# Last layer of a four-layer graph network: GpSimd paced by landed gathers instead of by marks from TensorE

## The reference, cut to what matters

```python
h = relu(edge_feat @ W1 + b1)                       # e x 64
w = (h @ W2 + b2).reshape(e, 4, 8, 8)               # e x 256
s_e = s[src]; v_e = v[src]                          # the gathered row: 8 + 24 numbers
m0 = ALPHA*(einsum(s_e*sh0, w_000) + C110*einsum(v_e, sh1, w_110))
m1 = ALPHA*(einsum(s_e, sh1, w_011) + einsum(v_e*sh0, w_101))
out0 = segment_sum(m0, dst) + SI_SCALE*(s @ si_w0)  # and out1 likewise
```

## Time and profile before

| | us |
|---|---|
| three runs | 7781.98, 7791.23, 7857.09 |
| median | 7791.23 |
| the profiled execution's own time | 7864.66 |
| its span in the profile | 7862.8 |
| last layer, first gather to the end of the last chunk | 4118.3 to 7849.8 |

### The profile page before, as it was taken

One profiled execution on the slowest core, in us unless ns is written; L12 is line 12 of the kernel. 1 busy time (PEld: TensorE's weight loads), 2 busy tenths in 40 slices (PEclk: granted clock), 3 DMA queues, 4 the chain that ended last, 5 costly groups with the idle time before them and its releaser, 6 DMA issues.

```text
span 7862.8 us, 118188 instructions
## 1 busy us (share of the span) xinstructions
PE 5606.6 (71%) x38929; PEld 4302.4 (55%) x38930; DVE 4286.2 (55%) x8297; ACT 3000.2 (38%) x7294; POOL 3946.9 (50%) x4168
## 2 busy tenths in 40 slices
PE   7477777777777775665674677777776777777677
PEld 3276777667666664333333455555555555555555
DVE  3355556665565561111103666666666666666677
ACT  4344444444444441000003444444444444444446
POOL 2355555555555555555204555555555555555553
PEclk6577777877877776776685667777776667776777
DMA  9433334444444447877880000000000000000000
GB/s 303 152 144 130 143 134 151 167 160 156 155 166 164 151 162 253 287 270 264 260 261 13 20 20 18 20 20 20 20 20 20 19 20 20 20 20 20 20 21 19
DMA packets 596643, 865.44 MB, mean 110 GB/s; under 512 B 170833, under 2 KB 418706, under 8 KB 579474
## 3 DMA queue, kind: packets, MB, share of 16 engines
q1 hardware_dynamic: 363858, 385.79, 15.5%
q10 hardware_dynamic: 99520, 406.06, 13.1%
q0 software_dynamic: 133120, 71.57, 4.9%
HBM read 455.19 MB, written 406.85 MB: 110 GB/s over the span
## 4 chain that ended last, share of the span: by engine, by line
PE 44%; another core or an unknown queue 18%; issue 16%; ACT 11%; DVE 8%; DMA 2%; ACTq 1%; DVEq 0%; SPq 0%
PE psum L1116 17%; PE psum L1066 9%; PE psum L1288 5%; PE psum L1174 5%; PE psum L1297 4%; ACT arena L768 3%; ACT arena L912 3%; ACT arena L798 2%; DVE arena L1970 2%; DVE arena L1956 2%; DVE arena L1948 2%; PE psum L1206 1%; DMA rel_table<-arena 1%; ACT arena L902 1%
## 5 line engine op out<-in xcount | busy, mean ns | idle before, releaser
L628 POOL DMA_INDIRECT gathered<-x_rows,idx x2048 | 1950.5, 952 | 2014.5 <-PE psum L1066 651.2
L628 POOL DMA_INDIRECT gathered<-rel_table,idx x2048 | 1933.6, 944 | 1664.4 <-issue 591.7
L1297 PE MATMUL psum<-w,arena 65*128 65x256 f32 x4096 | 1173.2, 439 | 331.5 <-DVE arena L1948 289.0
L797 ACT COPY arena<-psum 128x512 f32<-128x512 f32 x1024 | 603.4, 589 | 1552.0 <-PE psum L1116 1111.8
L1297 PEld LDWEIGHTS psum<-w,arena 65*128 65x128 f32 x4096 | 892.7, 225 | 497.3 <-DVE arena L1948 313.9
L1288 PE MATMUL psum<-arena,w 32*65 32x512 f32 x1024 | 575.5, 1061 | 656.1 <-ACT arena L896 398.2
L1066 PEld LDWEIGHTS psum<-arena 128*128 128x128 f32 x4096 | 885.2, 246 | 225.3 <-issue 203.8
L1116 PE MATMUL psum<-arena 64*128 64x128 f32 x8192 | 692.7, 326 | 420.7 <-ACT arena L798 253.2
L1066 PE MATMUL psum<-arena 128*128 128x184 f32 x4096 | 961.4, 398 | 3.9 <-DVE arena L1973 2.7
L1116 PE MATMUL psum<-table_out 64*128 64x128 f32 x8192 | 746.8, 349 | 239.5 <-ACT arena L798 173.6
L1116 PEld LDWEIGHTS psum<-arena 64*128 64x128 f32 x8192 | 630.9, 231 | 473.7 <-issue 250.2
(11 more groups left out here) (225 smaller groups left out, 5853.8 us busy)
## 6 DMA issues: line engine op xcount, KB each, us to landing
adj<-arena ACTq DMA_DIRECT2D x128, 2048.0 KB
arena<-adj SPq DMA_DIRECT2D x93, 2048.0 KB
counts<-arena ACTq DMA_DIRECT2D x128, 512.0 KB
arena<-counts SPq DMA_DIRECT2D x64, 1024.0 KB, 11.5
arena<-adj SPq DMA_DIRECT2D x40, 1024.0 KB
rel_table<-table_out ACTq DMA_DIRECT2D x32, 1024.0 KB
rel_table<-arena ACTq DMA_DIRECT2D x32, 1024.0 KB
gathered<-rel_table,idx POOLq DMA_INDIRECT x2048
```

The source lines that it names most:

```text
L628: pool.indirect_dma_start(gathered[:, s, j, :], None, rows[l], bass.IndirectOffsetOnAxis(ap=idx[:, s, j:j + 1], axis=0),).then_inc(group_i ...
L797: act.copy(w_to, made[:, 1]).then_inc(w_out, 1)
L1297: mm = pe.matmul(pair[g % 2][:, WN * q:WN * q + WN], hidden[:, s % 2, q, P * g:P * g + P], w2[:, :], start=True, stop=True)
```

## The change

The last layer's marks are taken out: `MARKS_3`, `MARK_TILES_3`, `CUTS_3` and `LEAD_3`, PE's five increments in every two chunks, and POOL's five waits for them. In their place POOL waits twice a chunk, ahead of its gathers 0 and 8, until the group of four gathers issued last has landed. Ahead of gather 8 that is group 1 of the same slot, ahead of gather 0 group 3 of the slot before. The amounts waited for are kept in eight registers, raised by 64 after each wait. The 64 gathers of the first round, the wait for `idx_in` ahead of each chunk, and the first layer's marks are as before.

```diff
-MARKS_3 = [({2}, (), {1}, {2}), ((), (), (), ())]
-MARK_TILES_3 = [(), (1, 9)]
-CUTS_3 = [0, 6, 12, 19, 25]
-LEAD_0, LEAD_LATE, LEAD_3 = 6, 6, 7
+RESTS_3 = (0, 8)
+LEAD_0, LEAD_LATE = 6, 6
...
+                def rows_landed(s, rest):
+
+                    last = (s - (rest == 0)) % SLOTS, (rest - 1) % TILES
+                    pool.wait_ge(group_in[last[0]][last[1] // GROUP], pool.snap(landed[s, rest]))
+                    pool.reg_add(landed[s, rest], landed[s, rest], 16 * GROUP)
+
+                def rests_3(s):
 
                     def pace(j):
 
-                        if s % 2 * TILES + j in CUTS_3:
-                            mark_passed()
+                        if j in RESTS_3:
+                            rows_landed(s, j)
                     return pace
...
-                        gather_chunk(3, s, marks_3(s))
+                        gather_chunk(3, s, rests_3(s))
...
-                    if q in marks:
-                        mm.then_inc(pe_mark, 1)
...
-                        mm = scatter(3, (s - 1) % SLOTS, (range(5), range(5, 11), range(11, TILES))[g - 1],
-                                     marks=MARK_TILES_3[s % 2])
+                        mm = scatter(3, (s - 1) % SLOTS, (range(5), range(5, 11), range(11, TILES))[g - 1])
```

More of the change, by code:

```diff
@@ L660, in marks_late @@
                         mark_passed()
-                def marks_3(s):
+                landed = {(s, rest): pool.alloc_register(f"landed_{s}_{rest}") for s in range(SLOTS) for rest in RESTS_3}
+                def rows_landed(s, rest):
[3 more added lines that the diff above has]
+                def rests_3(s):
                     def pace(j):
-                        if s % 2 * TILES + j in CUTS_3:
-                            mark_passed()
+                        if j in RESTS_3:
+                            rows_landed(s, j)
                     return pace
@@ L683, in _ @@
                     gather(2)
-                pool.reg_mov(mark, ROUNDS * by_round + MARKS_LATE * LATE + len(CUTS_3) * SLOTS // 2 + 1 - LEAD_3)
+                for s in range(SLOTS):
+                    for rest in RESTS_3:
+                        pool.reg_mov(landed[s, rest], 16 * GROUP * (1 + (s > 0 or rest > 0)))
                 pool.wait_ge(rows_out[2], 16)
@@ L1289, in hidden_units, with edge_weights @@
                               start=True, stop=True, tile_position=(F * q, 0)).then_inc(hidden_made, 1)
-            def edge_weights(c, s, g, marks):
+            def edge_weights(c, s, g):
                 if g == 0:
@@ L1307, in chunk3 @@
                 for g in range(GROUP):
-                    edge_weights(c, s, g, MARKS_3[s % 2][g])
+                    edge_weights(c, s, g)
                     if g == 1 and following:
```

## The result

| | before | changed |
|---|---|---|
| median of four runs each, us | 7792.19 | 7248.74 |
| lowest to highest, us | 7781.98 to 7857.09 | 7204.37 to 7264.39 |
| the profiled execution, us | 7864.66 | 7251.99 |

The changed kernel takes 0.9275 of the time of before, 95% interval 0.9225 to 0.9324: 543 us less on the chip of this measurement. On another chip the same kernel is slower than before by 8%; that is the second half of this document.

What follows compares the result with a forecast made beforehand. No engine was full; POOL's back-to-back gathers were taken to delay PE's semaphores. Chunks falling from 28.33 to 24.6 us, times 124, saved 463 us: 7402 profiled, about 7329 us as median, range 7130 to 7900.

Steps and rivals of the forecast that it cites:

- The state of things: Last layer: back-to-back POOL gathers delay PE's semaphores from about 5 us into a stretch until 1.7 to 2.6 us behind it.
- not the cause: Rival: PE's results are late for another reason and the gathers only coincide; 7791 us, chance 0.07.
- A stretch of eight and its pause clear: Last layer: eight gathers hold PE's semaphores 6.4 us instead of 12 to 13, and a 1.85 us pause just clears them.
- not cleared: Rival: 1.85 us is too short, a chunk's two stretches merge into one of about 21 us; 8740 us, chance 0.23 wholly or often.
- The pause: POOL's wait ahead of gathers 0 and 8: 1.05 us landing, 0.05 increment, 0.75 going on, 1.85 us in all.
- The upper bound of the prediction, 25.2: POOL's cycle in us a chunk if each pause took 2.9 us instead of 1.85.
- The reading that POOL has slack: Last layer: POOL's 23.1 us a chunk lies under the period, so nobody waits for its later gathers.
- How much of the hold-up a chunk feels: Last layer: DVE idles 4.8 us before group 2, repeating every 24.1 to 24.2 us; 24.6 us a chunk taken.
- The alternation of 21.6 and 37.9 us: Successive chunk periods of the kernel before, the long one holding two hold-up waits; the forecast was 24 to 25 us without it.
- The increments at zero: PE's five mark increments in two chunks ride on matmuls issued anyway; removal worth zero, at most 31 us for all 310.
- The sum: Last layer: (28.33 - 24.6) × 124 = 463 us off the profiled 7864.7, 7402; less 73 for the median, about 7329 us.

Runs made afterwards that it cites:

- stretches of sixteen: Changed kernel without its two waits a chunk, or with one, ahead of gather 0: 8212.49 and 8232.65 us on chip B, beside 7804.87 for the kernel before.
- B: Chip of four edits of the changed kernel: no pauses 8212.49, one pause 8232.65, gathers left out 6811.63, marks' increments kept 7260.99 us; kernel before 7804.87.
- A: Chip of the main result: changed kernel 7248.74 us beside 7792.19 for the kernel before; may be one of the other four chips.
- E: Chip of two edits of the changed kernel: waits for the group before 8385.16 us, ratio 1.0567; stretches of twelve 7811.15 us, ratio 0.9852.
- C: Chip of four edits of the changed kernel: four pauses 6605.11, first-round pauses too 6163.96, waits for the group before 5699.50, stretches of twelve 6047.43 us; kernel before 5700.81.
- D: Chip where the changed kernel ran again, unedited: 6149.80 us; with waits for the group before: 5696.00 us; kernel before 5703.32 us.
- The twelves: Changed kernel with three waits in two chunks, stretches of 12, 12 and 8 gathers: 6047.43 us (ratio 1.0620) on C, 7811.15 us (0.9852) on E.

## Why the prediction came out right, and where it did not

The forecast was 7329 us in 7130 to 7900, the result 7248.74. Point by point:

**The state of things: right for this chip.** Gathers back to back hold up PE's updates from some way into a stretch until 1.7 to 2.6 us behind it. The 5 us is a rough figure. In the changed kernel 290 of the 307 late updates are of matmuls that end over 5 us into a stretch. But of the recorded updates of matmuls that end 5 to 7 us in, less than a third are late, and of those 8 to 11 us in, six in seven. The prediction spoke of PE's updates alone; ACT's are late too, mostly in the stretches of sixteen (above), in those of eight 39 of 467, by up to 1.5 us. With the gathers gone the updates come at once and 449 us more are saved on the same chip (B: 7261 us with the marks' increments kept, 6812 without gathers), and with no or too short pauses the period is 31.2 to 31.8 us. The rival *not the cause* falls here, and its 7791 us with it. The rule of the Trainium skill (page "SBUF — State Buffer", section "Who interferes with whom") is that only VectorE and GpSimd contend and that TensorE never waits on anyone. It speaks of ports, and no trace here shows a port; what fails on A, B and E is what the prediction drew from it, that the gathers cannot delay PE's hand-offs. On C and D the traces agree with it.

**A stretch of eight and its pause clear: right, and narrowly.** The largest doubt, *not cleared* at 0.23, did not come true for eights: 1.99 us is as late as all but a few updates come, and the pause is 2.11. At the 1.85 us that the prediction had put down, 46 of the 307 late updates would have come after the pause's end. The twelves show the rival's mechanism. Its price was mis-sized: the prediction had merged two stretches into 36 us a chunk and 8740 us, the run without pauses has 31.29 and 8212 us. The 36 had counted a hold-up to 2.3 us behind a stretch that starts 2.3 after the release, with both later groups still to be done; in the trace the merged stretch lets some updates through late rather than none: group 2's weights reach DVE at 6016.53, inside the stretch, and only group 3 waits until behind it.

**The pause: 1.85 us predicted, 2.12 measured.** POOL's idle time in the table of waits is 782.2 + 266.2 us over 1933 gathers, 120.8 chunks: 8.68 us a chunk. Of that, 14 × 0.305 are the ordinary gaps, 0.15 comes of one gap of 0.92 us in four chunks, where the loop begins anew, and the two pauses are 2.12 us each in the mean. The term that was too small is the landing. The prediction put it at 1.05 us, though the packets in its own rows end by 6024.75, 0.91 us after 6023.84, and packets are not yet the update. On chip D, where every update is on record, the last update of the gather waited for comes 1.41 us after POOL has finished it (median), and POOL goes on 0.75 us later; that second term was right. The page puts the mean gather at 0.952 us, so POOL's cycle is 16 × 0.952 + 8.68 = 23.9 us, not 23.1. The upper bound of the prediction, 25.2, held it. The reading that POOL has slack is the one that wore thin: it has none, its cycle is half a microsecond above the period, and only the three chunks of lead hid that until the last ones.

**How much of the hold-up a chunk feels: 24.6 predicted, 23.4 measured.** The layout by hand gave 21.6 of DVE's own time and 3.0 more. The first was too large and the second a little too small: DVE's own is 20.1 (gathers left out), and what the hold-ups and the clock add is 3.3. The 21.6 was a period of before, 5994.97 to 6016.55, and had 1.5 us of waiting in it. The alternation of 21.6 and 37.9 us is gone, as said; half of all periods now lie between 23.1 and 24.0.

**The increments at zero:** not contradicted, but not shown to be zero either.

**The sum.** (28.33 - 23.41) × 124 = 610 us in the profiled executions, of which the slow end of the runs of before takes 70: 543 between the medians, 463 predicted. The term that was off is the period, by 1.19 us a chunk or 147 us. Against it stand 73 us that the prediction had taken off for the median of before. The changed kernel's own profiled execution lies on its median (7251.99 and 7248.74), so nothing had to be taken off. That these two of opposite sign left only 80 us between 7329 and 7249 is luck.

**What no rival had:** that the chip decides. The prediction priced its causes on one trace of one chip and took the hold-up as a property of the kernel. On D its own floor, POOL's cycle, is all that is left of the change, 3.6 us a chunk on top of 20.04, and before is the faster kernel there by 8%. Had the kernel been measured on D, its 6150 us would have been under the range's lower end.

## What to carry to other kernels

Where a trace shows results told late while another engine issues indirect DMAs, cut the stretch of them before asking for more overlap, and make the pause as long as the release takes: 2.1 us after eight gathers cleared it, the same after twelve failed for over half of the late results, and 0.3 us, and 0.72 us in the one case seen, did not clear at all. Price the pause first: it is spent on the issuing engine, and turned it here from 20.0 to 23.9 us a chunk, a bound in itself. And before such a pacing is kept, run it beside its baseline on more than one chip; the same edit was worth -7% on one and +8% on another. Of the versions that make all gathers, none was the fastest on both kinds.

## What the runs showed of the hardware that had not been expected

- **Two kinds of chip.** The kernel before takes 7792, 7805 and 7929 to 7934 us on A, B and E, and 5701 and 5703 us on C and D. The gathers take the same 0.94 us each at 1.25 us pitch on both. Before the last layer the difference is already there: its first gather is issued at 4128 us on A and at 3081 us on D (changed kernel). The first layer's gathers take 3542 us on A and 2561 on D, and from 500 to 2000 us a tenth of the recorded PE updates are over 2.4 us late on the one kind (before, A), 0.024 us on the other (D). What makes a chip of the one or the other kind was not found out; the traces show the lateness, not what the updates and the gathers share.
- **PE stands too.** In stretches of sixteen PE's own transposes come 1.5 to 1.9 us apart (473.5 us of "issue" in 2660 us). In stretches of eight this wait isn't among the list's first thirty. ACT's updates are late in stretches of sixteen as well; DVE's are not in the last layer's steady part, as far as they are recorded.
- **The clock follows.** PE's granted clock in the steady part is 0.65 without pauses, 0.74 with the change, 0.83 without gathers on chips with hold-ups, and 0.84 with gathers on a chip without: less standing goes with more clock, a mix of its two levels 1.2 and 2.4 GHz.
- **Landing.** A wait for the last gather's landing, and going on after it, takes POOL about 2.1 us on both kinds of chip (medians 2.11 on A, 2.17 on D), of which 1.41 is the landing and 0.75 the going on (D).
